# The mask of the causal diagonal, added to the first scores by quarters of the array instead of halves

## The reference

```python
logits = einsum('bihd,bjhd->bhij', q, k) * scale + SLOPES * (j - i)
logits = where(i >= j, logits, -inf)
x = layernorm(x + (softmax(logits) @ v) @ Wout)
gate, up = x @ wg.T, x @ wu.T
out = layernorm(x + (silu(gate) * up) @ wd.T)
```

## Time and profile before

| | |
|---|---|
| median of 3 runs | 2004.0 us (2002.14 to 2005.53) |
| profiled execution | 2002.88 us |
| its span in the trace | 2001.1 us |
| mean granted TensorE clock | 0.986 of full speed |
| TensorE matmul busy | 1896.9 us (95%) |
| VectorE, ScalarE, GpSimd busy | 1500.7, 1208.4, 1091.3 us |
| mask matmuls (`stair` moving, `turned` stationary) | 2560: 1536 long, 1024 short |

### The profile page before, as it was taken

How to read it: one execution, slowest core, us unless ns; L and a number is a source line. 1 busy time by engine, 2 the same in 40 slices (tenths; PEclk the granted TensorE clock), 3 DMA queues, 4 the chain that set the end, 5 groups by cost and what they waited for, 6 DMA issues and landing times.

```text
span 2001.1 us, 46915 instructions
## 1 busy us (share of the span) xinstructions
PE 1896.9 (95%) x18468; PEld 1457.8 (73%) x18468; DVE 1500.7 (75%) x2521; ACT 1208.4 (60%) x1999; POOL 1091.3 (55%) x2052
## 2 busy tenths in 40 slices
PE   5889999999999999999999999999999999999986
PEld 4556777777777777777777777777777777777666
DVE  5567787777787777878777878777778777777745
ACT  1655666566666666666666666666666656666653
POOL 0234655555565555565555565555566556556565
PEclk7999999999999999999999999999999999999998
DMA  5464544444444444445445454444454444444320
GB/s 202 148 198 138 171 150 146 162 157 144 158 157 152 154 152 158 149 153 168 139 150 172 139 168 153 144 162 160 133 170 157 143 158 157 151 156 141 109 76 27
DMA packets 164860, 299.29 MB, mean 150 GB/s; under 512 B 33920, under 2 KB 84864, under 8 KB 152064
## 3 DMA queue, kind: packets, MB, share of 16 engines
q1 hardware_dynamic: 164448, 295.24, 45.1%
q10 hardware_dynamic: 192, 1.05, 0.2%
HBM read 175.64 MB, written 119.54 MB: 148 GB/s over the span
## 4 chain that ended last, share of the span: by engine, by line
PE 69%; DVE 12%; ACT 10%; POOL 7%; issue 2%; DMA 1%; SPq 0%; POOLq 0%; DVEq 0%; ACTq 0%
PE pair L574 68%; ACT probs L795 6%; DVE row_max L874 4%; DVE row_max L877 4%; DVE x1t_lo L862 2%; POOL probs L993 2%; POOL attn_lo L1013 2%; ACT pv_t L803 2%; POOL attn L1008 2%; POOL h_lo L1000 1%; ACT x1t_hi L775 1%; PE pair L577 1%; DVE row_max L879 0%; DMA probs<-L_attn_Wqkv 0%; DVE staged_lo L862 0%
## 5 line engine op out<-in xcount | busy, mean ns | idle before, releaser
L795 ACT ACTIVATE probs<-pair 128x1024 f32<-128x1024 f32 x640 | 620.7, 1030 | 320.9 <-PE pair L574 320.4
L993 POOL TENSOR_SCALAR_AFFINE_SELECT probs<-probs 128x256 f32<-128x256 f32 (+1 forms) x896 | 380.1, 440 | 650.9 <-ACT probs L795 646.7
L1000 POOL TENSOR_TENSOR h_lo<-h_fulls,h_hi 128x256 fp32r<-128x256 f32 x384 | 276.9, 743 | 129.4 <-ACT h_hi L827 127.9
L574 PE MATMUL pair<-probs,v_ones 128*32 128x512 f32 (+3 forms) x4096 | 328.5, 439 | 4.4 <-ACT probs L795 1.5
L574 PE MATMUL pair<-q_rows,k_rows 64*128 64x512 f32 (+3 forms) x2048 | 315.3, 365 | 8.3 <-ACT probs L795 0.8
L877 DVE TENSOR_REDUCE row_max<-pair 128x2 f32<-128x1024 f32 x256 | 312.4, 1220 | 12.7 <-PE pair L574 8.0
L574 PE MATMUL pair<-k_rows,q_rows 63*128 63x512 f32 (+3 forms) x2048 | 296.9, 347 | 23.4 <-DVE row_max L877 15.2
L879 DVE TENSOR_REDUCE row_max<-pair 128x8 f32<-128x1024 f32 x256 | 311.8, 1218 | 0.0
L574 PEld LDWEIGHTS pair<-k_rows,q_rows 63*128 63x128 f32 x2048 | 165.2, 186 | 168.6 <-DVE row_max L877 81.4
L874 DVE TENSOR_REDUCE row_max<-pair 128x4 f32<-128x1024 f32 x128 | 156.7, 1224 | 123.8 <-PE pair L574 123.8
L819 ACT ACTIVATE h_fulls<-pair 128x256 f32<-128x256 f32 x384 | 145.0, 378 | 153.7 <-PE pair L574 149.9
(11 more groups left out here) (89 smaller groups left out, 3411.8 us busy)
## 6 DMA issues: line engine op xcount, KB each, us to landing
q_rows<-bounce SPq DMA_DIRECT2D x192, 256.0 KB
k_rows<-bounce SPq DMA_DIRECT2D x192, 256.0 KB
bounce<-staged_hi SPq DMA_DIRECT2D x128, 256.0 KB, 2.5
bounce<-staged_lo SPq DMA_DIRECT2D x128, 256.0 KB, 2.8
pv_bounce<-pv_t SPq DMA_DIRECT2D x128, 256.0 KB, 2.0
x_sb<-L_attn_x SPq DMA_DIRECT2D x32, 512.0 KB, 4.2
attn<-pv_bounce SPq DMA_DIRECT2D x64, 256.0 KB
recips<-recip_bounce SPq DMA_DIRECT2D x64, 256.0 KB
```

What stands on the lines that cost most here:

```text
L574: return tensor.matmul(o, lhs, rhs, start=start, stop=stop, skip_group_check=True, **kw)
L795: scalar.activation(probs[g][:, tile, :, :], pair[:, :, :], ACT.Exp, scale=scale).then_inc(s_exp, 1)
L993: made = pool.affine_select(out=diagonal, in_=diagonal, compare_op=ALU.is_ge, fill=0.0, base=0, pattern=[[0, diagonal.shape[1]], [1, P]], ...
L1000: pool.tensor_tensor(h_lo[:, m, :], h_full[(n_split_h[step] - 1) % H_BUFFERS][:, :], h_hi[:, m, :].bitcast(F32), ALU.subtract).then_inc(s_ ...
```

## The change

The four mask matmuls of an F step become four of 64 rows and 64 columns, one for each quarter of the array: head `s` selects the rows, key half `c` the columns, and with them the partitions of PSUM that are written. The stationary operand is a 64 x 64 identity (`eye`), the same for all; the quarter of keys 64 to 127 and queries 0 to 63 is no longer touched by them. It is masked by the coarse mask instead, whose stretches are now exactly 64 tokens: `COARSE_ROWS` goes from 10 to 7. The three freed rows hold zeros. The tables are smaller: `squares` has 3 planes instead of 4, and one start-up cast shrinks from 256 to 64 columns. Counts of matmuls, steps, waits and all other code stay.

```diff
-ALIBI_ROWS, COARSE_ROWS = 4, 10
+ALIBI_ROWS, COARSE_ROWS = 4, BANK // HALF - 1
...
-    stretch = np.arange(tokens) // -(-tokens // COARSE_ROWS)
+    stretch = np.arange(tokens) // HALF
...
-    stair[HALF - 1] = MASKED
-    turned = np.zeros((2, HALF, P), np.float32)
-    turned[0, :, :HALF] = turned[1, :, :HALF] = turned[1, :, HALF:] = np.eye(HALF)
-    turned[:, HALF - 1, :] = 0
-    turned[1, HALF - 1, :HALF] = 1
-    planes = [turned[0], turned[1], np.concatenate([stair, stair], 1)]
-    return rows, np.stack([identity] + [np.concatenate([table, table]) for table in planes], 1)
+    eye = np.eye(HALF, dtype=np.float32)
+    planes = [np.tile(table, (2, 2)) for table in (eye, stair)]
+    return rows, np.stack([identity] + planes, 1)
...
-        turned, stair = sb("turned", [P, 2, P], BF16), sb("stair", [P, 2, HALF], BF16)
+        eye, stair = sb("eye", [P, HALF], BF16), sb("stair", [P, 2, HALF], BF16)
...
                     for c in range(2):
-                        made = both(lambda s: halves[:, s, masked, c, :], lambda r: turned[r:r + HALF, c, :],
-                                    lambda r: stair[r:r + HALF, 0:n, :], False, c == 1)
+                        for s in range(2):
+                            made = mm(halves[c * HALF:(c + 1) * HALF, s, masked, c, :], eye[s * HALF:(s + 1) * HALF, :],
+                                      stair[s * HALF:(s + 1) * HALF, 0:n, :], False, True, tile_position=(s * HALF, c * HALF))
                     made.then_inc(s_first, 1)
```

More of the change, by code:

```diff
@@ L436, in build @@
         down_f = [flat(h_fulls, 0, hidden), flat(results, 0, hidden)]
-        squares_sb = flat(x1[0], 0, 4 * P).rearrange("p (s n) -> p s n", n=P)
+        squares_sb = flat(x1[0], 0, 3 * P).rearrange("p (s n) -> p s n", n=P)
         split_tiles = {
@@ L851, in _ @@
             vector.tensor_copy(ident[:, :], squares_sb[:, 0, :]).then_inc(s_ready, 1)
-            vector.tensor_copy(turned[:, :, :], squares_sb[:, 1:3, :]).then_inc(s_ready, 1)
-            vector.tensor_copy(stair[:, :, :], squares_sb[:, 3, :].rearrange("p (b n) -> p b n", b=2)).then_inc(s_ready, 1)
+            vector.tensor_copy(eye[:, :], squares_sb[:, 1, 0:HALF]).then_inc(s_ready, 1)
+            vector.tensor_copy(stair[:, :, :], squares_sb[:, 2, :].rearrange("p (b n) -> p b n", b=2)).then_inc(s_ready, 1)
             silu_halves = 0
```

## The result

The change makes the kernel slower. The median went from 2003.07 us (4 runs, 2001.82 to 2005.53) to 2047.3 us (4 runs, 2046.42 to 2047.73): ratio 1.0214, 95% interval 1.0201 to 1.0227. The forecast was 2053, its range 2025 to 2105. The profiled execution's span grew from 2001.1 to 2045.8 us, at the same mean TensorE clock of 0.986, so the clock plays no part.

What follows compares the result with a forecast made beforehand. The prediction took TensorE as the bound, with VectorE's row maxima ruling part of each stretch. Of 1.74 us added per stretch 0.80 stays; times 63 that is 50 us, and 2002.88 + 50 = 2053 us, range 2025 to 2105.

Steps and rivals of the forecast that it cites:

- A new array shape costs 0.09: At each change of TensorE's array shape the array stands empty for 0.09 us; bounds 0 and 0.10.
- Entry E: From the last k_rows pair to the mask's end in an F step: 0.07 us more long, 0.10 short.
- Exit X: After the mask, weights of a following S step come later by 0.14 us long, 0.12 short; 0 where V follows.
- (1): F0 to F1 add 0.29 us ahead of V(-2,1,0); the wait for S0's exponent absorbs 0.12, 0.17 stays.
- (2, 3): Delay grows to 0.39 us behind F2, 0.42 behind F3 (0.04 to spare there), 0.49 behind F4.
- (4): VectorE's two row maxima rule until F7; extra time of F5 (0.22 us) and F6 (0.21) fits; 0.49 stays.
- (5): F7 adds 0.10 us and F8 0.07 + 0.14: 0.80 when V(-1,0,1) ends.
- (6): F9's 0.21 us on TensorE is hidden beside ScalarE's copy and two exponents; 13 us in all if not.
- A: Quarters need no emptying of the array: 1988 us, or no measurable change (-3 us); chance 0.11.
- B: Nothing is absorbed, VectorE's and ScalarE's waits move along: 2113 us; chance of this or most of it 0.10.
- C: Weights or matmuls of quarters in one array half go one after another, about 0.10 us an entry: 2097; chance 0.07.
- D: Only the way into the mask's shape empties the array, not the way back: 26 us, 2029; chance 0.07.

Runs made afterwards that it cites:

- halves run: Against the changed kernel: mask matmuls back to 64 rows by 128 columns, coarse mask in stretches of 64 kept; 2003.34 us.
- run with one quarter: Against the changed kernel: c = 0 mask matmuls back to 64*128, only c = 1 still by quarters (64*64); 2069.04 us.
- run beside the path: Against the kernel with 64*128 mask matmuls and the new coarse mask: quarters in F5, F6 and F9 alone; 2003.69 us.

## Why the prediction was right

*A new array shape costs 0.09.* Right, and now shown for 64*64: weights come 0.10 behind the end of the stream on the way in. The halves run leaves the shape of the mask matmuls alone to blame, the run with 66 columns for c = 0 clears the quick load and the number of columns, and the run with one quarter clears the number of quarter matmuls; I know of no cause that is left. That the array runs empty in these 0.10 us is an inference from when the weights come. The Trainium skill's sentence in TensorEngine Tiling (Array Packing), Key Properties, that a change of tiling mode drains the engine, agrees with these runs. It gives no price; here it is about 0.1 us each way.

*Entry E.* Predicted 0.07 long, 0.10 short. F7 to V gives 0.084 for a short one (0.456 - 0.372). For a long one V's weights come 0.327 us behind F3's last k_rows pair, where they came 0.276 behind (medians): 0.05. F8 to S7 gives 0.200 for E and X together, against 0.21. The term that was too large is the weight load: +0.04, taken at 0.80 ns a column from f32 loads. From the last of the mask's four loads (0.01 behind 1022.03) to the load of S at 1022.21 it is 0.17, of which 0.053 is the stream and 0.09 the emptying: 0.02 to 0.03 is left for 64 bf16 columns, and against the quick load it is +0.011, as the run with one quarter shows. The price of 0.053 us for 64 columns that the prediction gives beside its sum is twice too high as well; the measurement decides.

*Exit X.* Predicted 0.12 to 0.14 where S follows, 0 where V follows: S1 is 0.195 later behind F0 and V(-1,0,0) only 0.084 behind F7, a difference of 0.11 for a short one; for a long one 0.200 - 0.05 leaves 0.15.

*What absorbs it.* (1) Predicted 0.17 at V(-2,1,0), measured 0.090: E was too large twice, and in the kernel before F1's two heads ran 0.03 apart, which the change evened out. (2, 3) Predicted 0.39 behind F2 and 0.42 behind F3, measured 0.290 and 0.317; the steps between are as predicted. (4) Predicted 0.49 at F7, measured 0.372; F5 and F6 add nothing, as the run with quarters in F5, F6 and F9 shows by itself; but F5's part is taken up ahead of S5 by the wait for an exponent, which the prediction did not see, and not ahead of F6. (5) Predicted 0.80 at V(-1,0,1), measured 0.650. (6) F9's part is hidden: S9 is 0.109 late in that run and its time is unchanged.

The sum is 0.65 x 63 = 41 us instead of 50; the profiled executions differ by 44.7. From the first weights of one S0 to those of the next it is 29.43 us on average before and 30.12 after, 0.69 more: over the 62 full stretches that makes 43 of the 44.7. The time ahead of the loop is 0.7 us shorter, and that behind the last unit's scores, where no mask matmul stands, 2.6 us longer (94.8 and 97.5 us). These 2.6 need not come from the change: with 66 columns and no quarter at all the same piece takes 97.3 us, with halves 94.8. So a part of the nearness to 2053 may be luck. The term that was mis-sized is the weight load inside E: some 0.02 us in each of seven entries, most of the 0.15; F1's heads are another 0.03.

Of the signs named ahead, the `eye` loads came 0.149 us behind the start of the last k_rows pair, the four mask matmuls within 0.01 of each other, the wait ahead of F7 went; the weights of S came 0.17 behind the last mask matmul, where 0.14 was said, and two stretches lie 0.69 further apart instead of 0.8.

*The rivals.* A falls by the result and by the `eye` loads, which come 0.10 behind the stream; what a free mask could have won is known from the run without it, 31 us. B falls by the result (2047 against 2113), and by the run beside the path: by B's own prices it adds 0.64 us a stretch, and the time is unchanged. C: the four loads start within 0.01 us. D: both directions cost, as the two equal gaps of the run with one quarter show.

## What to carry to other kernels

Count the changes of array shape along TensorE's order, not only the columns that each matmul streams: here each one cost 0.1 us of emptiness, and kept the next weights from loading ahead, while the stream that a quarter saved was 0.03 to 0.07. Even beside a change of shape that is there anyway, behind F3 and F7 where V follows, four quarters cost 0.05 and 0.08 us more than four halves. It would take more matmuls of the small shape in a row for them to pay; no run here has that.

Price an edit at the place where it stands. The same 0.2 us in an F step counted in full at F2 and F8, and not at all at F5, F6 and F9; a step held by another engine can lose up to its wait for nothing, and has no time to win. And do not add up busy times to judge such an edit: the mask's group became 19 us cheaper while the kernel lost 44.

## What the runs showed of the hardware that was not expected

- A bf16 load of 128 columns (the profile's 96 ns) did not start before the running f32 stream had ended (0.05 behind the start of a 128-column pair), while a load of 66 columns (107 ns) started with that pair. Swapping the one for the other made the kernel 5 us faster (0.9975), though the load itself is slower. The Trainium skill, in TensorE: Matmul & The Clock Gate, Weight-path perf modes, ties the fast load to 128 columns of a type that is not FP32. Both shapes here fit that; which of the two loads is drawn ahead was measured.
- Doing the same for the second load gave the gain back (0.9997), in the steps where the stream before it is short.
- Loads of 64 bf16 columns took some 0.024 us until their matmul could stream (an estimate: 0.011 more than the 0.013 from one quick load to the next), against 0.11 from load to load for 128 f32 columns.
